# Reordering ACT and DVE between the seventh merged-weight product and the end of batch 0 in a two-layer LoRA kernel

## What is computed

```
x = x + L0(x):   x @ W0.T + ((x @ A0[i0[b]]) @ B0.T) * 0.5
x = x + L1(x):   x @ W1.T + bias + ((x @ A1[i1[b]]) @ B1[i1[b]]) * 2.0
x is (8, 256, 1024) float32, W0 and W1 are 1024 x 1024, A0 (5, 1024, 32), A1 (32, 1024, 16)
```

## Time and profile before

| | us |
|---|---|
| median of 3 runs | 312.31 (311.42 to 313.07) |
| the profiled execution | 311.56 |
| its span, first to last instruction | 309.9 |
| PE / DVE / ACT / POOL busy in the span | 292.8 / 195.5 / 132.4 / 63.3 |

### The profile page before, as it was taken

One profiled execution on the slowest core, in us unless ns is written; L12 is line 12 of the kernel. 1 busy time (PEld: TensorE's weight loads), 2 busy tenths in 40 slices (PEclk: granted clock), 3 DMA queues, 4 the chain that ended last, 5 costly groups with the idle time before them and its releaser, 6 DMA issues.

```text
span 309.9 us, 3802 instructions
## 1 busy us (share of the span) xinstructions
PE 292.8 (94%) x1323; PEld 238.6 (77%) x1323; DVE 195.5 (63%) x294; ACT 132.4 (43%) x213; POOL 63.3 (20%) x82
## 2 busy tenths in 40 slices
PE   8999999998649999499999999999999999999995
PEld 4788787886338888388888888888888888888784
DVE  2689999778797999987427328327337336346120
ACT  4681254764955029444414423423423424425100
POOL 1500000500104710006105115114124133132000
PEclk9999999999978999899999999999999999999999
DMA  6996000200301100501811811711612612601003
GB/s 192 364 372 243 0 0 2 70 0 2 135 0 35 52 19 0 169 27 61 253 42 44 256 48 43 247 52 66 223 53 76 213 53 87 201 36 68 34 8 127
DMA packets 13750, 30.79 MB, mean 99 GB/s; under 512 B 2210, under 2 KB 3618, under 8 KB 12708
## 3 DMA queue, kind: packets, MB, share of 16 engines
q1 hardware_dynamic: 12708, 28.46, 27.3%
q0 software_dynamic: 1024, 2.10, 2.4%
HBM read 20.06 MB, written 8.39 MB: 92 GB/s over the span
## 4 chain that ended last, share of the span: by engine, by line
PE 70%; DVE 19%; ACT 7%; issue 3%; DVEq 0%; ACTq 0%
PE bank L943 48%; PE bank L933 4%; PE bank L814 3%; PE bank L818 2%; PE bank L823 2%; PE bank L950 2%; PE bank L949 2%; DVE rA L671 2%; PE bank L856 2%; DVE sf L593 1%; DVE sc L593 1%; DVE rA L680 1%; DVE M L684 1%; PE bank L913 1%; DVE MM L593 1%
## 5 line engine op out<-in xcount | busy, mean ns | idle before, releaser
L427 ACT ACTIVATE zo<-bank 128x512 f32<-128x512 f32 x32 | 19.1, 598 | 93.2 <-PE bank L943 63.5
L779 DVE TENSOR_TENSOR zo<-bank,zo 128x512 f32<-128x512 f32 x32 | 22.1, 692 | 54.3 <-PE bank L950 32.3
L943 PE MATMUL bank<-MM,X 128*128 128x512 f32 x192 | 46.2, 389 | 0.0
L943 PEld LDWEIGHTS bank<-MM,X 128*128 128x128 f32 x192 | 36.0, 188 | 7.5
L943 PE MATMUL bank<-sa,SH 128*128 128x512 f32 x96 | 24.8, 410 | 3.9 <-ACT zo L427 3.9
L332 POOL TENSOR_TENSOR xraw<-xraw 128x512 f32<-128x512 f32 x8 | 10.3, 1290 | 81.1 <-DVE X L593 81.1
L943 PEld LDWEIGHTS bank<-sa,SH 128*128 128x128 f32 x96 | 19.1, 199 | 8.5 <-ACT zo L427 4.3
L593 DVE TENSOR_TENSOR X<-xraw,X 128x1024 fp32r<-128x1024 f32 x16 | 19.4, 1220 | 7.6 <-ACT X L427 7.6
L593 DVE TENSOR_TENSOR SH<-xraw,SH 128x512 fp32r<-128x512 f32 x32 | 23.7, 781 | 0.0
L943 PE MATMUL bank<-sb,SH 128*128 128x512 f32 x96 | 23.2, 390 | 0.2 <-ACT zo L427 0.2
L943 PE MATMUL bank<-sc,SH 128*128 128x512 f32 x96 | 23.3, 391 | 0.0
(11 more groups left out here) (180 smaller groups left out, 556.3 us busy)
## 6 DMA issues: line engine op xcount, KB each, us to landing
xraw<-xT SPq DMA_DIRECT2D x8, 1024.0 KB, 5.4
out<-zo SPq DMA_DIRECT2D x32, 256.0 KB, 2.0
rB<-w1T SPq DMA_DIRECT2D x16, 256.0 KB, 9.9
rA<-w SPq DMA_DIRECT2D x15, 256.0 KB, 9.4
Rraw<-Rg SPq DMA_DIRECT2D x16, 128.0 KB, 3.8
rawA<-la SPq DMA_DIRECT2D x8, 128.0 KB, 2.2
Rraw<-lbs POOLq DMA_DIRECT2D x16, 64.0 KB, 3.2
rawA<-las POOLq DMA_DIRECT2D x8, 64.0 KB, 5.5
```

Of the source, the lines that this page charges most:

```text
L427: return eng.activation(o, i, ACT.Copy, scale=scale)
L779: ins = eng.tensor_tensor(zo[z][:, :], bank[bk][:, :], zo[z][:, :], ALU.add)
L943: ins = mm(bk[:, :], x(px, k), m(pm, k), start=(start and n == 0 and k == 0), stop=(stop and n == 2 and k == H - 1), skip_group_check=True)
```

## The change

The same instructions are issued, with these differences:

- Order of ACT and DVE from m7 on: T3, A1D and WS go ahead of the rests of S3 and T3; U2s is placed between the S3/T3 copies; P5s ahead of and between the B22 copies; M11 and S4 earlier; T4 later (behind BQ(1) on ACT, between the halves of xL(0) on DVE); M22's split behind UL(0), just ahead of V4.
- GTS(1) and BT(1) on ACT no longer stand behind T4; BR(1) on DVE no longer behind M22's rests.
- V2 and V3 exchange slots: V3 now in a, V2 in b, with the waits exchanged in `last`; V3's split comes ahead of V2's and of M21's.
- Batch 0's four token sums run on DVE instead of POOL, between the rests of x, a and g and in the M12/V loop. POOL keeps batch 0's load of the adapter rows (`v0`) and the sums of the batches 1 to 7.
- In batch 0 on PE, U (the low-rank product of batch 1) comes last, behind P4, instead of between D and P3. The ACT and DVE orders of batch 0 are written out for this; those of the batches 1 to 7 stay.

```
--- before.py
+++ after.py
@@ -60,6 +60,8 @@
 
 def lora_kernel(nc, xT, w0, w1T, la, lb, las, lbs, bias, i0, i1, out):
     def batch_steps(b):
+        if b == 0:
+            return ["P1", "P5", "P6", "P2", "P7", "D", "P3", "P4", "U"]
         if b + 1 < B:
             return ["P1", "P5", "P6", "P2", "P7", "D", "U", "P3", "P4"]
         return ["P1", "P5", "P6", "D", "P7", "P2", "P3", "P4"]
@@ -109,45 +111,47 @@
     for k in range(H):
         act_prog += h([("T1", k, k + 1), ("S1", k, k + 1)])
         dve_prog += [("S1", k)] + l_([("T1", k, k + 1), ("S1", k, k + 1)])
-    act_prog += [("U2s", i) for i in range(H)]
+    dve_prog += [("T3", k) for k in range(H)] + [("A1D",), ("WS",)]
     for k in range(H):
         act_prog += h([("S3", k, k + 1), ("T3", k, k + 1)])
-        dve_prog += [("T3", k)] + l_([("S3", k, k + 1)]) + l_([("T3", k, k + 1)])
-    act_prog += h(two("A22")) + [("A1DH",), ("WSH",)] + h(two("B22")) + [("P5s", i) for i in range(H)]
-    dve_prog += l_(two("A22")) + [("A1D",), ("WS",)] + l_([("B22", 0, 2)]) + [("A1DL",), ("WSL",)] + l_([("B22", 2, 4)])
-    dve_prog += [("U2P5", i) for i in range(H)] + [("BR", 0), ("TT",), ("TM",)]
-    act_prog += [("TMH",), ("B1H",)] + [("BQ", 0, q) for q in (1, 2, 3)] + h(two("T4")) + h(two("M11"))
-    dve_prog += [("TML",), ("B1L",)] + l_(two("T4")) + [("M22", i) for i in range(H)] + l_(two("M11"))
-    act_prog += h(two("S4")) + [("GTS", 1)] + h(two("M22")) + [("BT", 1)]
-    dve_prog += l_(two("S4")) + l_(two("M22")) + [("BR", 1)] + [("RG", g, c) for g in range(2) for c in range(2)]
-    act_prog += [("GR", j) for j in range(2)] + [("BQ", 1, q) for q in (1, 2, 3)]
+        dve_prog += l_([("S3", k, k + 1), ("T3", k, k + 1)])
+        if k in (0, 1):
+            act_prog += [("U2s", 2 * k), ("U2s", 2 * k + 1)]
+    act_prog += h(two("A22")) + [("A1DH",), ("WSH",), ("P5s", 0), ("P5s", 1)] + h([("B22", 0, 2)])
+    act_prog += [("P5s", 2), ("P5s", 3)] + h([("B22", 2, 4)])
+    dve_prog += l_(two("A22")) + [("A1DL",), ("WSL",)] + [("U2P5", i) for i in range(H)] + l_(two("B22"))
+    dve_prog += [("BR", 0), ("TT",), ("TM",)]
+    act_prog += h(two("M11")) + [("TMH",), ("B1H",)] + h(two("S4")) + [("BQ", 0, q) for q in (1, 2, 3)]
+    dve_prog += l_(two("M11")) + [("TML",), ("B1L",)] + [("M22", i) for i in range(H)] + l_(two("S4"))
+    act_prog += [("GTS", 1), ("BT", 1)] + [("GR", j) for j in range(2)] + [("BQ", 1, q) for q in (1, 2, 3)] + h(two("T4"))
+    dve_prog += [("BR", 1)] + [("RG", g, c) for g in range(2) for c in range(2)]
     act_prog += [("xH", 0, 0), ("xH", 0, 1), ("aH", 0), ("gH", 0)]
-    dve_prog += [("xL", 0, 0), ("xL", 0, 1), ("aL", 0), ("gL", 0)]
+    dve_prog += [("xL", 0, 0)] + l_(two("T4")) + [("xL", 0, 1), ("SA", 0, 1), ("aL", 0), ("SA", 0, 3), ("gL", 0)]
 
 
     for i in range(H):
-        dve_prog += [("M12", i), ("V1", i), ("V3", i), ("V2", i)]
+        dve_prog += [("M12", i)] + ([("SA", 0, 2)] if i == 0 else [("SA", 0, 4)] if i == 1 else [("RL", 0)] if i == 2 else [])
+        dve_prog += [("V1", i), ("V3", i), ("V2", i)]
         act_prog += h([("V1", i, i + 1)])
         if i > 0:
             dve_prog += l_([("V1", i - 1, i)])
         if i == 1:
             act_prog += [("RH", 0)]
-            dve_prog += [("RL", 0)]
-    dve_prog += l_([("V1", 3, 4)])
-    act_prog += [("SH", 0, 1), ("SH", 0, 2)] + h(two("V2")) + [("SH", 0, 3), ("SH", 0, 4)]
-    dve_prog += [("SL", 0, 1), ("SL", 0, 2)] + l_(two("V2")) + [("SL", 0, 3), ("SL", 0, 4)]
-    act_prog += h([("M21", 0, 1), ("M21", 1, 2), ("M21", 2, 3), ("V3", 0, 2), ("V3", 2, 4), ("M21", 3, 4)])
-    for i in range(H):
-        if i == 3:
-            dve_prog += l_(two("V3"))
-        dve_prog += l_([("M21", i, i + 1)]) + [("V4", i)]
-    act_prog += [("UH", 0)] + [("E1", 0)] + h(two("V4"))
-    dve_prog += [("U2", 0), ("UT", 0), ("UL", 0)] + l_(two("V4"))
-
-    for b in range(B):
+    act_prog += [("SH", 0, n) for n in (1, 2, 3, 4)] + h(two("V3"))
+    dve_prog += [("SL", 0, 1)] + l_([("V1", 3, 4)]) + [("SL", 0, n) for n in (2, 3, 4)] + l_(two("V3"))
+    act_prog += h([("M21", 0, 1), ("M21", 1, 2), ("M21", 2, 3)] + two("V2") + [("M21", 3, 4)])
+    dve_prog += l_([("M21", 0, 1), ("M21", 1, 2), ("M21", 2, 3)] + two("V2") + [("M21", 3, 4)])
+    act_prog += [("UH", 0), ("E1", 0)] + h(two("M22"))
+    dve_prog += [("U2", 0), ("UT", 0), ("UL", 0)] + l_(two("M22")) + [("V4", i) for i in range(H)]
+
+    act_prog += [("aH", 1), ("gH", 1), ("xH", 1, 0), ("E2", 0)] + h([("V4", 0, 2)]) + [("E3", 0)] + h([("V4", 2, 4)])
+    act_prog += [("xH", 1, 1)] + [("SH", 1, n) for n in range(1, 5)] + [("E4", 0), ("UH", 1), ("RH", 1)]
+    dve_prog += [("C11", 0)] + l_([("V4", 0, 2)]) + [("C22a", 0), ("C22b", 0)] + l_([("V4", 2, 4)])
+    dve_prog += [("aL", 1), ("gL", 1), ("xL", 1, 0), ("xL", 1, 1)] + [("SL", 1, n) for n in range(1, 4)]
+    dve_prog += [("C12", 0), ("SL", 1, 4), ("U2", 1), ("UT", 1), ("UL", 1), ("RL", 1)]
+    for b in range(1, B):
         more = b + 1 < B
-        if b > 0:
-            act_prog.append(("E1", b))
+        act_prog.append(("E1", b))
         if more:
             act_prog += [("aH", b + 1), ("gH", b + 1), ("xH", b + 1, 0), ("E2", b), ("xH", b + 1, 1)]
             dve_prog += [("aL", b + 1), ("gL", b + 1), ("xL", b + 1, 0), ("C11", b), ("xL", b + 1, 1)]
@@ -239,7 +243,7 @@
 
 
         HOME = {"A12": "b", "B21": "d", "A11": "a", "B11": "c", "S2": "e", "T2": "f", "S3": "a", "T3": "f", "S1": "c",
-                "A22": "d", "B22": "e", "T1": "b", "S4": "a", "T4": "b", "M22": "c", "V1": "f", "V2": "a", "V3": "b",
+                "A22": "d", "B22": "e", "T1": "b", "S4": "a", "T4": "b", "M22": "c", "V1": "f", "V2": "b", "V3": "a",
                 "V4": "d"}
         FROM = {"S3": "A11", "T3": "B12", "S1": "A21", "T1": "B11", "S4": "A12", "T4": "B21", "M22": "A22", "V3": "A21",
                 "V4": "A22"}
@@ -268,9 +272,12 @@
         d_z = [sem(f"d_z{i}") for i in range(4)]
 
         pool_prog = ["id0", "ident", "mk0", "mk1", "mask", "wz"]
-        pool_prog += ["slot", "Rraw", "ones"] + [("SA", 0, n) for n in (1, 3, 2, 4)]
+        pool_prog += ["slot", "Rraw", "ones", "v0"]
         pool_prog += [("SA", b, n) for b in range(1, B) for n in (1, 3, 2, 4)]
-        pool_at = Order(pool_prog).at
+        pool_at = Order([n for n in pool_prog if n != "v0"]).at
+
+        def x_quarters():
+            return (xraw[:, k:k + H, c:c + 128] for c in (0, 128) for k in (0, H))
 
         block = ctx.enter_context(nc.Block())
 
@@ -310,6 +317,7 @@
                         "o r n -> (o r) n")).then_inc(d_Rv, 16)
 
             tt = eng.tensor_tensor
+            xa1, xa2, xb1, xb2 = x_quarters()
             for op in pool_prog[6:]:
                 if op == "slot":
                     eng.wait_ge(s_pe, pe_at["BP", 1])
@@ -322,11 +330,13 @@
                         eng.memset(STA[i][:, :].bitcast(F32), 0.0)
                         eng.memset(STB[i][:, :].bitcast(F32), 0.0)
                     ins = eng.memset(ones[:, :], 1.0)
+                elif op == "v0":
+                    load_v(0)
+                    continue
                 else:
                     _, b, n = op
                     if n == 1:
                         load_v(b)
-                    xa1, xa2, xb1, xb2 = (xraw[:, k:k + H, c:c + 128] for c in (0, 128) for k in (0, H))
                     if n == 1:
                         eng.wait_ge(s_dve, dve_at["xL", b, 1])
                         ins = tt(xb2, xb1, xb2, ALU.add)
@@ -442,7 +452,7 @@
 
                 last = {"S3": ("GT", 0), "T1": ("GT", 0), "S1": ("BP", 0), "A22": ("BP", 0), "B22": ("m6", H - 1),
                         "T3": ("m6", H - 1), "S4": ("m7", H - 1), "T4": ("m5", H - 1), "M22": ("GT", 1),
-                        "V1": ("BP", 1), "V2": ("m3", H - 1), "V3": ("m4", H - 1), "V4": ("m4", H - 1)}
+                        "V1": ("BP", 1), "V2": ("m4", H - 1), "V3": ("m3", H - 1), "V4": ("m4", H - 1)}
                 if q in last:
                     eng.wait_ge(s_pe, pe_at[last[q]])
                 elif q == "M11":
@@ -562,10 +572,11 @@
                     ins = copy(slot[:, :, 64 + RA:64 + U], G[:, :, RB * b:RB * (b + 1)])
                 elif k == "SH":
                     _, b, n = op
-                    eng.wait_ge(s_pool, pool_at["SA", b, n])
                     if b == 0:
+                        eng.wait_ge(s_dve, dve_at["SA", 0, n])
                         eng.wait_ge(s_pe, pe_at["m3", H - 1])
                     else:
+                        eng.wait_ge(s_pool, pool_at["SA", b, n])
                         eng.wait_ge(s_pe, pe_at[{1: "P5", 2: "P6", 3: "P7", 4: "P3"}[n], b - 1])
                     ins = copy(SH[:, n - 1, 0, :, :], s_raw(n))
                 elif k == "UH":
@@ -746,6 +757,13 @@
                     eng.wait_ge(s_act, act_at["xH", b, h])
                     a = slice(0, H), slice(0, T)
                     ins = rest(xhl(b, h, 1, *a), xraw[:, H * h:H * (h + 1), :], xhl(b, h, 0, *a))
```

(7 more changed lines are left out.)

## The result

The changed kernel takes **301.62 us** (median of 4 runs, 301.33 to 303.66) against 312.69 (311.42 to 313.75) for the kernel before on the same chip: ratio 0.966, 95% interval 0.961 to 0.972. The profiled execution took 301.54, its span 299.9 against 309.9. The forecast was 301.0 (297.5 to 304.3), with a gain of 11.3; the spans differ by 10.0, the medians by 11.1.

A forecast was written before the change was run, and what follows sets the result against it. PE, busy 94%, bounds by its work plus holes ending on ACT or DVE. Lead 13.9 less waits given back: net 11.3; 311.56 - 11.3 = 300.2 profiled, plus 0.75 for the median: 301.0 us, range 297.5 to 304.3.

The forecast's parts named there:

- Ahead of m3: PE before batch 0: holes of 1.42, 3.17 and 3.79 us go; m3 starts at 84.6 instead of 96.30.
- DVE's chain to E1: DVE and ACT work before P6 of batch 0: E1 at 115.9, P6 at 116.6, a 2.8 us hole remains.
- the lower of my two bounds: Batch 0's four token sums on DVE: 2.2 or 2.4 us in all; the walk took 2.4.
- Rival (b): DVE becomes the bound, sums at the upper bound, lower clock behind the 2.8 us hole: gain 8.8, 303.5; chance 0.26.
- The swap: Exchanging V2's and V3's slots lets V3 be copied early, its slot free after m3; adds no instruction.
- The clock behind the 2.8 us hole: Lower clock in batch 0's P6: it takes 4.46, 1.0 later, but P3's wait of 1.2 swallows it.
- P3 wants C22a. On DVE ahead of it ...: Batch 0: DVE's queue ahead of C22a ends it at 127.5, so P3 waits 1.2 us.
- The forecast wait of 1.2: PE ahead of batch 0's P3: 1.2 us waiting for C22a, formerly hidden by U's 1.9 us.
- P5 of batch 1: It waits 0.5 to 1.4 us for C12(0), behind SL rests beside POOL sums; upper end taken, start 140.0.
- "U(1) moved behind P4 costs nothing itself": End of batch 0 on PE: moving batch 1's U behind P4 costs nothing, the same 1.9 us.
- Rival (e): Slower: load of x(2) issued 4.7 us after P1(1) starts, delaying P7(1), repeating every batch; about 314.5; chance 0.03.
- bracket (a): Whole kernel: the forecast itself, gain 10.4 to 12.3 us, 300.0 to 302.0; chance 0.52.

The follow-up runs named there:

- gts_only: Kernel before, with only GTS(1) and BT(1) earlier on ACT, BR(1) and RG earlier on DVE, M11, S4, M22 behind: 309.59 us against 311.95, ratio 0.993.
- pool_sums: Changed kernel with batch 0's four token sums on POOL again: 302.61 us, ratio 0.976 to the kernel before.
- no_swap: Changed kernel with V2 in slot a and V3 in slot b again, waits exchanged with them: 301.07 us, ratio 0.967 to the kernel before.
- fill: Changed kernel with eleven more matmuls, results unread, on PE between P5 and P6 of batch 0: 300.57 us, ratio 0.963 to the kernel before.
- v2_first: Changed kernel with V2's split ahead of M21's on both engines, UH and E1 right behind V2's copies: 300.92 us, ratio 0.962 to the kernel before.
- u_early: Changed kernel with batch 1's U between D and P3 again, its x and adapter splits ahead of C22a: 301.02 us, ratio 0.964 to the kernel before.
- v2_c22: v2_first plus C22a of batch 0 ahead of V4's rests on DVE: 301.60 us, ratio 0.970 to the kernel before.
- c12_first: Changed kernel with C12 of batch 0 ahead of batch 1's three SL rests in DVE's queue: 300.05 us, ratio 0.961 to the kernel before.

## Why the prediction was right, and where it was off

- **Ahead of m3: right.** GT(1) at 71.91 (71.7), GTS(1) at 77.61 (77.4), transposes from 81.05 (81.1), m3 at 84.76 (84.6). gts_only shows what this took: the queues of both engines, not two moved copies.
- **DVE's chain to E1: right.** The four sums took 0.68 to 0.69 each, the lower of my two bounds, and V3 beside them 0.69 instead of 1.67:

```profile
92.60 0.69 DVE L766 TENSOR_TENSOR xraw<-xraw 128x512 f32<-128x512 f32 x1
...
96.26 0.69 DVE L691 TENSOR_TENSOR rA<-rA,rA 128x512 f32<-128x512 f32 x1
```

  From GT(1), P6 starts at 44.9 as forecast. pool_sums puts the exchange of POOL for DVE at 1.3 us, against 3.6 - 2.4 = 1.2. Rival (b)'s dear sum did not appear.
- **The swap: wrong reason.** Both slots were free before their copies (m4 is over at 106.52, V3 is copied from 110.23); no_swap shows no difference.
- **The clock behind the 2.8 us hole: right size, wrong consequence.** Rival (b) gave P6 1.0 us more and had P3's wait swallow it. P3's wait swallowed nothing. The step that failed is "P3 wants C22a. On DVE ahead of it ...": I walked DVE's queue and left out the other thing that C22a waits for, E3. In the changed kernel it is E3 that comes last; ACT, then DVE:

```profile
127.40 0.60 ACT L437 ACTIVATE zo<-bank 128x512 f32<-128x512 f32 x1 [1.78 <-PE bank L961]
```

```profile
128.10 1.49 DVE L797 TENSOR_TENSOR zo<-bank,zo 128x512 f32<-128x512 f32 x2 [0.65 <-ACT zo L437]
```

  P7 ends, E3 copies, C22a adds, P3 starts: 1.03 us behind D, whenever P7 ends, as long as DVE is ready. So a delay of PE ahead of P7 goes on to P3, and fill, which removes it, gains 0.7. It gains no more, because the two limits lie close together. In fill and in v2_first C22a follows DVE's queue without idle time; first fill, then v2_first:

```profile
127.08 1.48 DVE L797 TENSOR_TENSOR zo<-bank,zo 128x512 f32<-128x512 f32 x2
```

```profile
129.89 1.48 DVE L797 TENSOR_TENSOR zo<-bank,zo 128x512 f32<-128x512 f32 x2
```

  Both are 55.44 behind GT(1), against 56.19 in the changed kernel, and P3 starts at 56.2 in both, although v2_first has P2 1.8 us earlier. So the walk of DVE's queue was nearly right (P3 forecast at 55.9), and with P6 at full clock E3 ends only 0.1 ahead of C22a (126.98 in fill). The forecast wait of 1.2 lay near the measured 1.03 for this reason, and not because the wait had been understood; what the missing E3 cost is the 0.75 us of the clock. That is the larger part of the 1.15 us by which P5 of batch 1 came later than forecast (141.15, forecast 140.0); another 0.2 is GT(1)'s own later start, and 0.2 is left (68.5 in fill, 68.3 forecast).
- **P5 of batch 1: right.** It waits 1.01 (0.5 to 1.4 forecast), and the row shows the exclusion that I took for the upper end; a rest SL on DVE, and POOL's sums beside it:

```profile
135.60 1.22 DVE L604 TENSOR_TENSOR SH<-xraw,SH 128x512 fp32r<-128x512 f32 x1 [2.08 <-ACT SH L437]
...
134.98 1.30 POOL L345 TENSOR_TENSOR xraw<-xraw 128x512 f32<-128x512 f32 x1
136.35 1.62 POOL L348 TENSOR_TENSOR xraw<-xraw 128x512 f32<-128x512 f32 x1
```

- **"U(1) moved behind P4 costs nothing itself": true only by itself.** U's 1.9 us used to cover E3 and C22a. In u_early a wait of 1.53 ahead of U takes the place of the 1.03 ahead of P3, and the gain lies at P5 of batch 1, because the split of x also starts the sums earlier. The choice that cost about 1 us is the late split of x with C12 behind the rests SL.
- **Rival (e)** did not happen: the load of x(2) lay 4.5 us behind P1 of batch 1 (141.73, 137.23), and no wait followed. P5 of batch 1 itself, behind its hole, took 2.86 from start to start instead of 2.72; from its end on the kernels run alike.

**How near the number was.** Profile against profile the gain is 10.0, not 11.3: 1.15 us were lost by P5 of batch 1 and 0.14 in it. 10.0 lies below the 10.4 at which the forecast's own bracket (a) ends. The forecast for the profiled execution was 300.2, and it took 301.54. The median came within 0.6 of 301.0 because I had added 0.75, by which the median of the runs before lay above their profile; in the changed kernel the median lies 0.08 above it. That half of the error is hidden by the spread of the runs is luck.

## What to carry to other kernels

When engines run hand-written orders, walk every instruction on the chain to **all** its waits, also those that are not last in the trace before: a reordering makes another one the last, and a wait tied to the bound engine's own output (P7, E3, C22a, P3) absorbs no delay of that engine while the helper is ready. A lead on the bound engine is worth only what the helper engines can follow: v2_first had P2 1.8 us ahead of fill, and P3 started at 56.2 in both. The two halves of the change gave 2.6 and 5.6 apart, and 10.0 together. Compare small edits from a common event in the trace, not from the start of the span, where the loading of data varied by more than the edits were worth.

## What the runs showed of the hardware

- A PE hole of 2.79 us lowered the granted clock (0.53 behind it), as did 2.87 in v2_first; one of 2.52 in v2_c22 did not. In other executions of the same kernels, of which only the span and the mean granted clock are recorded, the mean was 1.000 in one of four of no_swap (299.95 us) and of u_early (299.90) and in two of four of v2_first, and 0.992 to 0.994 in two of four of v2_c22. So it seems to vary between executions whether a hole of this size lowers the clock; no trace shows it. The price, against P2 at 48.6 in fill, varied between profiles of kernels alike up to there: 0.6 us in no_swap, 0.8 in the changed kernel, 1.2 in c12_first.
- Eight fp32 transposes of 128x128 ran in 0.79 us at clock 1.00, and in 1.6 at 0.50.
- A POOL sum begun just behind a DVE rest with two SBUF inputs took 2.36 us instead of 1.29, and the second of DVE's two rests stood behind it, so both engines lose.
